# A second attention re-cast on the context's 64 columns: folded weights, raw contexts summed

## What is computed

```
x = x + tanh(g_xattn[0]) * attention0(layernorm(x), ctx)      # 16 heads, causal self part and cross part
x = x + tanh(g_ffn[0])   * moe_top2_capacity(layernorm(x))    # 8 experts, 320 slots each, F = 512
x = x + tanh(g_xattn[1]) * attention1(layernorm(x), ctx, ctx)
x = x + tanh(g_ffn[1])   * moe_dense(layernorm(x))            # 8 experts, all rows, F = 128

def attention1(query, key, value):          # one head of width 128, key and value are 64 wide
    q = query @ Wq + bq
    k = key @ Wk + bk
    v = value @ Wv + bv
    return softmax(q @ k.T, axis=-1) @ v
```

## Time and profile before

| | |
|---|---|
| time, median of 3 runs (lowest, highest) | 335.41 us (332.91 to 335.91) |
| the profiled execution: span from first to last instruction | 337.6 us |
| TensorE matmul busy in it | 312.9 us (93%) |
| TensorE weight load (overlaps) | 189.6 us (56%) |
| VectorE, ScalarE, GpSimd busy | 220.8, 194.1, 115.7 us |
| granted TensorE clock, mean | 0.995 |

### The profile page before, as it was taken

How to read it: one execution, slowest core, us unless ns; L and a number is a source line. 1 busy time by engine, 2 the same in 40 slices (tenths; PEclk the granted TensorE clock), 3 DMA queues, 4 the chain that set the end, 5 groups by cost and what they waited for, 6 DMA issues and landing times.

```text
span 337.6 us, 7474 instructions
## 1 busy us (share of the span) xinstructions
PE 312.9 (93%) x2891; PEld 189.6 (56%) x2891; DVE 220.8 (65%) x532; ACT 194.1 (57%) x410; POOL 115.7 (34%) x200
## 2 busy tenths in 40 slices
PE   8998969989999999899977999999996899999995
PEld 3545733334443434344666677777794357776665
DVE  4998798888989889676242052333321956779665
ACT  3468588978888889787266733323336265512221
POOL 6476732327334333231775003444442211110000
PEclk9999999999999999999997999999999999999999
DMA  7855995940437006240441580000002200000101
GB/s 174 199 110 160 175 213 132 209 90 10 153 110 209 5 5 188 70 124 2 109 157 35 133 212 10 21 18 19 22 12 70 71 0 2 1 2 0 31 3 31
DMA packets 35827, 27.83 MB, mean 82 GB/s; under 512 B 5627, under 2 KB 33070, under 8 KB 35792
## 3 DMA queue, kind: packets, MB, share of 16 engines
q1 hardware_dynamic: 33965, 25.04, 29.7%
q0 software_dynamic: 1280, 1.88, 1.7%
q10 hardware_dynamic: 547, 0.44, 0.5%
HBM read 11.89 MB, written 5.26 MB: 51 GB/s over the span
## 4 chain that ended last, share of the span: by engine, by line
PE 73%; ACT 7%; DVE 6%; issue 5%; POOL 5%; DMA 2%; SPq 0%; DVEq 0%; POOLq 0%; ACTq 0%
PE psum L1682 11%; PE psum L1876 11%; PE psum L1957 8%; PE psum L1624 5%; PE psum L1648 5%; PE psum L1945 4%; PE psum L1864 4%; ACT qk_r L948 3%; PE psum L1814 2%; POOL rows_in L797 2%; PE psum L1651 2%; PE psum L2060 2%; PE psum L2052 1%; PE psum L1575 1%; PE psum L1869 1%
## 5 line engine op out<-in xcount | busy, mean ns | idle before, releaser
L1213 DVE TENSOR_REDUCE nmax<-psum 128x2 f32<-128x1024 f32 (+2 forms) x88 | 102.0, 1216 | 11.6 <-PE psum L1624 10.3
L948 ACT ACTIVATE parts<-psum 128x512 f32<-128x512 f32 (+1 forms) x88 | 45.2, 566 | 8.6 <-PE psum L1648 7.7
L1876 PE MATMUL psum<-p_more,kcat 128*128 128x320 f32 (+2 forms) x160 | 40.2, 396 | 0.9 <-DVE p_more L1346 0.7
L819 POOL DMA_INDIRECT rows_back<-qcat,back_at x24 | 22.9, 952 | 50.3 <-ACT qcat L981 43.1
L1876 PEld LDWEIGHTS psum<-p_more,kcat 128*128 128x128 f32 x160 | 26.1, 190 | 9.1 <-issue 0.9
L1350 DVE TENSOR_TENSOR qcat<-psum,qk_r 128x320 f32<-128x320 f32 (+2 forms) x40 | 16.6, 422 | 22.1 <-ACT qk_r L989 13.5
L989 ACT ACTIVATE qk_r<-psum 128x320 f32<-128x320 f32 (+2 forms) x40 | 15.2, 384 | 24.5 <-PE psum L1876 21.5
L1682 PE MATMUL psum<-parts,v_aug 128*18 128x256 f32 (+1 forms) x352 | 28.5, 369 | 0.0
L1957 PE MATMUL psum<-h_t,kcat 128*128 128x512 f32 x60 | 28.1, 594 | 0.0
L1682 PE MATMUL psum<-qk_r,v_aug 128*18 128x256 f32 (+1 forms) x160 | 27.4, 373 | 0.0
L1648 PE MATMUL psum<-qcat,kcat 64*128 64x256 bf16 x256 | 24.7, 271 | 1.9 <-ACT p_more L948 0.8
(11 more groups left out here) (249 smaller groups left out, 630.4 us busy)
## 6 DMA issues: line engine op xcount, KB each, us to landing
kcat<-parts SPq DMA_DIRECT2D x18, 192.0 KB, 3.8
qcat<-parts SPq DMA_DIRECT2D x21, 128.0 KB, 3.6
kcat<-ones_b SPq DMA_DIRECT2D x8, 192.0 KB, 4.6
kcat<-in_L_ffn_wi_gate_dram SPq DMA_DIRECT2D x6, 256.0 KB, 4.5
kcat<-in_L_ffn_wi_up_dram SPq DMA_DIRECT2D x6, 256.0 KB, 4.8
kcat<-in_L_ffn_wo_dram SPq DMA_DIRECT2D x6, 256.0 KB, 5.0
parts<-in_L_ffn_w_dram SPq DMA_DIRECT2D x3, 512.0 KB, 5.6
rows_in<-zeros SPq DMA_DIRECT2D x1, 1290.0 KB, 5.7
```

The lines of the kernel that those rows point to most:

```text
L819: pool.indirect_dma_start(out=rows_back[:, :], out_offset=bass.IndirectOffsetOnAxis(ap=back_at[0:m, e, t:t + 1], axis=0), in_=eo[0:m, e % ...
L948: act.activation(p_slots[u % NPT][:, 0:w], s2_bank(s2_place[u])[:, 0:w], ACT.Exp, scale=SCALE).then_inc(p_in, 1)
L1213: dve.tensor_reduce(dst[:, :, n * g:n * (g + 1)], src.rearrange("p (r q k) -> p r q k", r=PAR, q=n), AX.X, ALU.max, negate=True).then_inc( ...
L1876: ins = pe.matmul(gate_up_bank(i, m)[:, 0:end - first], w_t[e][:, m, f * P:(f + 1) * P], xs_t[:, e % 2, first:end], start=True, stop=True)
```

## The change

Scores are q k.T = (h Wq + bq)(ctx Wk + bk).T. The change folds Wq Wk.T into one matrix of 128 x 64 (`mk`) with bq Wk.T as a bias column, so that a "query" has 64 numbers and is matched with the raw context; what is left of a query's score, the same for all its keys, is the offset h (Wq bk) + bq bk, which is computed for every tile (`off`, one column) and only rounds the subtracted maximum (`s1_bias`). On the other side p @ (ctx Wv + bv) = (p @ ctx) Wv + bv: the raw context rows are summed and then multiplied by Wv.

- `context` with its 8 banks and copies goes, and so do k1_t and v1. `fold_weights1` comes: two transposes, 2 unread matmuls, four small matmuls, three ScalarE instructions; then 8 unread matmuls (`N_UNREAD_ROWS`).
- The two tiles of a batch lie on rows 0 to 63 and 64 to 127: queries of odd tiles go to output partitions 64 on; the turned context is copied to partitions 64 to 127 by a DMA; `scores1(b)` does both tiles, each on its row half, into banks 0, 1 or 4, 5. `sums1(b)`: 4 x 2 matmuls, context rows (128 x 64) as weights, a tile's sums on each column half, into bank 6. `values1(b)`: one matmul of 256 columns of both tiles by a block-diagonal Wv (`w1_v2`), into bank 7.
- Each of ScalarE's `take_queries` has a second instruction for the offsets; VectorE gets a small instruction behind each maximum, and a copy of the sums (`take_sums1`).
- The order is now by batches on TensorE, ScalarE and VectorE. GpSimd gets a memset of w1_v2 among its constants, a scale of bv, and x + bv over all rows (into x1_sb) between rstd(2) and rstd(3). SyncE loads bv and Wv twice in place of two loads, and issues two DMAs (context rows again, and the copy of c_t) behind the loads of the last layer's weights.

```diff
-w1_v = sb("w1_v", [DC + 1, D])
+w1_v2 = sb("w1_v2", [P, 2 * D])
+b1v = sb("b1v", [P, D])
...
-c_t = sb("c_t", [DC + 1, NC * P])
+c_t = sb("c_t", [P, NC * P])
...
-k1_t = q_place(AFTER_HH + 6 * D, NC * P)
...
-v1 = q_place(AFTER_HH + 6 * D + NC * P, NC * D).rearrange("p (t d) -> p t d", t=NC)
...
+TURN1_BANK, MK_BANK = 3, 4
+N_UNREAD_ROWS = 8
+N_IN_LATE = 11
...
+def s1_bank(t):
+    return bank(4 * (t // QT % 2) + t % QT)
...
-        for w, n in ((w1_k, "k"), (w1_v, "v")):
-            load(w[0:DC, :], a["L1_xattn_W" + n])
-            load(w[DC:DC + 1, :], a["L1_xattn_b" + n].unsqueeze(0))
+        load(w1_k[0:DC, :], a["L1_xattn_Wk"])
+        load(w1_k[DC:DC + 1, :], a["L1_xattn_bk"].unsqueeze(0))
+        load(b1v[:, :], a["L1_xattn_bv"].partition_broadcast(P))
+        sp.wait_ge(w1v_zero, 1)
+        for t in range(QT):
+            load(w1_v2[t * DC:(t + 1) * DC, t * D:(t + 1) * D], a["L1_xattn_Wv"])
...
+    sp.dma_start(ctx_rows, c_in).then_inc(ctx_again, 16)
+    sp.dma_start(c_t[DC:2 * DC, :], c_t[0:DC, :]).then_inc(ctx_again, 16)
...
+    pool.memset(w1_v2[:, :], 0.0).then_inc(w1v_zero, 1)
...
+        link(pool.tensor_scalar(b1v[:, :], b1v[:, :], tanh_g[:, 1:2], None, ALU.mult))
...
     rstd(2)
+    pool.tensor_tensor(x1_sb[:, :, :], x_sb[:, :, :], b1v[:, :].unsqueeze(1).to_broadcast([P, NT, D]),
+                       ALU.add).then_inc(xv_in, 1)
     rstd(3)
...
-    for j in range(2 * B):
-        act.wait_ge(kv1_full, j + 1)
-        src = bank(KV1_BANK[j])
-        if j < B:
-            act.activation(k1_t[:, j * BANK:(j + 1) * BANK], src, ACT.Copy).then_inc(kv1_act, 1)
-        else:
-            dst = v1[:, CT * (j - B):CT * (j - B + 1), :]
-            act.activation(dst, src.rearrange("p (t d) -> p t d", t=CT), ACT.Copy).then_inc(kv1_act, 1)
+    act.wait_ge(gw_in, 1)
+    act.activation(bq_wide, zeros[:, 0:D], ACT.Identity, bias=b1_col[:, :]).then_inc(bq_in, 1)
+    act.wait_ge(mk_full, 1)
+    act.activation(w1_turned, bank(TURN1_BANK)[:, 0:D + DC + 1], ACT.Copy).then_inc(mk_act, 1)
+    act.wait_ge(mk_full, 2)
+    act.activation(mk, bank(MK_BANK)[:, 0:MK_OFF + 1], ACT.Copy).then_inc(mk_act, 1)
...
     def take_queries(s):
         first, end = BACK[s]
+        n = (end - first) // QT
         act.wait_ge(q1_full, s + 1)
-        act.activation(q1_of(first, end), bank(Q1_BANK)[:, 0:(end - first) * P], ACT.Identity,
-                       bias=b1_col[:, :]).then_inc(q1_act, 1)
+        act.activation(q1_t[:, first // QT:end // QT, :], bank(Q1_BANK)[:, 0:n * P]
+                       .rearrange("p (b q) -> p b q", b=n), ACT.Identity,
+                       bias=mk[:, MK_BIAS:MK_BIAS + 1]).then_inc(q1_act, 1)
+        act.wait_ge(off1_full, s + 1)
+        act.activation(s1_off[:, first:end], bank(OFF1_BANK)[:, 0:end - first], ACT.Identity,
+                       bias=mk[:, MK_OFF:MK_OFF + 1]).then_inc(off1_in, 1)
     def exp1(t):
+        b = t // QT
         act.wait_ge(nm1_in, t + 1)
-        if t >= 2:
-            act.wait_ge(p1t_full, t - 1)
-        act.activation(p1[:, t % 2, :], bank(t % 2), ACT.Exp, bias=s1_nmax[:, t:t + 1],
+        if b >= 2:
+            act.wait_ge(p1t_full, t - 2 * QT + 1)
+        act.activation(p1[:, b % 2, t % QT, :], s1_bank(t), ACT.Exp, bias=s1_bias[:, t:t + 1],
                        accum_out=s1_sum[:, t:t + 1]).then_inc(p1_in, 1)
     def take_turned1(t):
+        b = t // QT
         act.wait_ge(p1t_full, t + 1)
-        if t >= 2:
-            act.wait_ge(o1_full, t - 1)
-        act.activation(p1_t[:, t % 2, :], bank(2 + t % 2), ACT.Copy).then_inc(p1t_in, 1)
+        if b >= 2:
+            act.wait_ge(u1_full, b - 1)
+        act.activation(p1_t[:, b % 2, t % QT, :], bank(2 + t % 2), ACT.Copy).then_inc(p1t_in, 1)
     for e in range(E):
         take_weights1(e)
     take_rows(0)
     take_queries(0)
     take_rows(1)
-    exp1(0)
     take_queries(1)
-    for t in range(NT):
-        if t + 1 < NT:
-            exp1(t + 1)
+    for t in range(QT):
+        exp1(t)
+    for t in range(QT):
         take_turned1(t)
-        if t == ROWS_AT:
-            take_rows(2)
-        if t == QUERIES_AT:
-            take_queries(2)
+    take_rows(2)
+    take_queries(2)
+    for b in range(1, B):
+        for t in range(QT * b, QT * b + QT):
+            exp1(t)
+        if b > 1:
+            for t in range(QT * b - QT, QT * b):
+                take_turned1(t)
+    for t in range(NT - QT, NT):
+        take_turned1(t)
     dense_experts()
...
     def max1(t):
         dve.wait_ge(sc1_full, t + 1)
-        dve.tensor_reduce(s1_nmax[:, t:t + 1], bank(t % 2), AX.X, ALU.max, negate=True).then_inc(nm1_in, 1)
+        link(dve.tensor_reduce(s1_nmax[:, t:t + 1], s1_bank(t), AX.X, ALU.max, negate=True))
+        if t in (0, BACK[1][0], BACK[2][0]):
+            dve.wait_ge(off1_in, [first for first, _ in BACK].index(t) + 1)
+        dve.scalar_tensor_tensor(out=s1_bias[:, t:t + 1], in0=s1_nmax[:, t:t + 1], scalar=s1_off[:, t:t + 1],
+                                 in1=s1_off[:, t:t + 1], op0=ALU.subtract, op1=ALU.add).then_inc(nm1_in, 1)
+    def maxima1(b):
...
+    def take_sums1(b):
+        dve.wait_ge(u1_full, b + 1)
+        dve.tensor_copy(u1_t[:, b % 2, :], bank(U1_BANK)[:, 0:P]).then_inc(u1_in, 1)
+    def add_values(b):
+        dve.wait_ge(o1_full, b + 1)
+        if b == 0:
+            dve.wait_ge(xv_in, 1)
+        for t in range(QT * b, QT * b + QT):
+            dve.scalar_tensor_tensor(out=x1_sb[:, t, :], in0=bank(O1_BANK)[:, t % QT * D:(t % QT + 1) * D],
+                                     scalar=s1_rec[:, t:t + 1], in1=x1_sb[:, t, :],
+                                     op0=ALU.mult, op1=ALU.add).then_inc(x3_in, 1)
+        for t in range(QT * b, QT * b + QT):
             row_statistics(t)
-    def reciprocal1(t):
-        dve.wait_ge(p1_in, t + 1)
-        link(dve.reciprocal(s1_rec[:, t:t + 1], s1_sum[:, t:t + 1]))
-        link(dve.tensor_tensor(s1_rec[:, t:t + 1], s1_rec[:, t:t + 1], tanh_g[:, 1:2], ALU.mult))
+    def reciprocal1(b):
+        tiles = slice(QT * b, QT * b + QT)
+        dve.wait_ge(p1_in, QT * b + QT)
+        link(dve.reciprocal(s1_rec[:, tiles], s1_sum[:, tiles]))
+        link(dve.tensor_scalar(s1_rec[:, tiles], s1_rec[:, tiles], tanh_g[:, 1:2], None, ALU.mult))
...
     add_back(2, 1)
-    max1(0)
     statistics(2, 2, x_sb)
-    for t in range(NT):
-        if t + 1 < NT:
-            max1(t + 1)
-        reciprocal1(t)
-        if t == 0:
-            normalise(2, 2, x_sb)
-        if t >= 1:
-            add_values(t - 1)
-        if t == NT - 2:
-            normalise(3, 0, x1_sb)
-    add_values(NT - 1)
+    maxima1(0)
+    normalise(2, 2, x_sb)
+    maxima1(1)
+    reciprocal1(0)
+    take_sums1(0)
+    maxima1(2)
+    reciprocal1(1)
+    add_values(0)
+    maxima1(3)
+    take_sums1(1)
+    reciprocal1(2)
+    add_values(1)
+    normalise(3, 0, x1_sb)
+    take_sums1(2)
+    reciprocal1(3)
+    add_values(2)
+    take_sums1(3)
+    add_values(3)
...
-                    if e == 0:
-                        pe.wait_ge(kv1_act, 2 * B - 2)
                     pe.wait_ge(xt_in, e + 1)
                 if i == 1:
                     pe.wait_ge(wt_in[0], 3 * E)
-                    pe.wait_ge(kv1_act, 2 * B)
+                    pe.wait_ge(mk_act, 2)
...
-    def context(j):
-        if j >= 4:
-            pe.wait_ge(kv1_act, j - 3)
-        elif KV1_BANK[j] in W_LAST:
-            pe.wait_ge(wt_in[0], W_LAST[KV1_BANK[j]] + 1)
-        dst = bank(KV1_BANK[j])
-        if j < B:
-            ins = pe.matmul(dst, w1_k[:, :], c_t[:, j * SC:(j + 1) * SC], start=True, stop=True)
-        else:
-            for c in range(CT):
-                tok = (CT * (j - B) + c) * P
-                ins = pe.matmul(dst[:, c * P:(c + 1) * P], c_t[:, tok:tok + P], w1_v[:, :],
-                                start=True, stop=True)
-        ins.then_inc(kv1_full, 1)
-    for j in range(2 * B):
-        context(j)
+    def unread(n):
+        for _ in range(n):
+            pe.matmul(bank(0), ones_b[:, 0:P], ones_b[:, 0:BANK], start=True, stop=True)
+    def fold_weights1():
+        dst = bank(TURN1_BANK)
+        pe.transpose(dst[:, 0:D], w1_q[:, :], ident[:, :])
+        pe.transpose(dst[:, D:D + DC + 1], w1_k[:, :], ident[0:DC + 1, 0:DC + 1]).then_inc(mk_full, 1)
+        unread(2)
+        pe.wait_ge(mk_act, 1)
+        pe.wait_ge(bq_in, 1)
+        pe.wait_ge(wt_in[0], W_LAST[MK_BANK] + 1)
+        wq, wk, dst = w1_turned[:, 0:D], w1_turned[:, D:D + DC + 1], bank(MK_BANK)
+        pe.matmul(dst[:, 0:DC + 1], wq, wk, start=True, stop=True)
+        for t in range(QT):
+            pe.matmul(dst[t * DC:(t + 1) * DC, MK_BIAS:MK_BIAS + 1], wk[:, 0:DC], b1_col[:, :], start=True, stop=True)
+        pe.matmul(dst[:, MK_OFF:MK_OFF + 1], bq_wide, wk[:, DC:DC + 1], start=True, stop=True).then_inc(mk_full, 1)
+    fold_weights1()
+    unread(N_UNREAD_ROWS)
...
     def turn_back(s):
         first, end = BACK[s]
         if s > 0:
```

(103 more changed lines are left out.)

51 lines of the change are left out of this document (29 added, 22 removed).

## The result

| | before | after |
|---|---|---|
| time, median of 5 runs (lowest to highest) | 333.36 us (332.88 to 335.91) | 342.76 us (340.37 to 343.54) |
| ratio after to before | | 1.0254, 95% interval 1.0205 to 1.0303 |
| span of a profiled execution, mean clock | 337.6 us, 0.995 | 338.6 us, 0.988 |

The account below looks back on a forecast made before the run. TensorE was taken as the bound in the context's stage and second attention. Terms +0.5 - 2.45 + 1.65 = -0.3 on the 337.6 us span gave 337.3, less 2.2 to the plain runs' median: 335.1 us, range 331.8 to 338.9.

Parts of the forecast that it names:

- Step 2, the fold's -2.45: Context's stage: with the fold replacing the context's matmuls, the first row transpose starts 2.45 us earlier.
- rival D: Context's stage: the fold doesn't move the experts, giving 337.55 us; chance 0.05.
- Step 4, GpSimd's x + bv: Second attention: the addition costs nothing, or at most 0.5 us if it slows VectorE's normalising beside it.
- Step 4, the order: Second attention: walking through the engines' new instruction orders puts the dense start 1.65 us later.
- both gaps: Second attention: TensorE idles 1.7 us before sums1(1) (first gap) and 1.9 us before values1(2) (second gap).
- Step 3: Second attention: TensorE's own work falls by 2.3 us net, with halves running beside each other.
- Rival B: Second attention, scores1 and sums1: float32 halves don't overlap, +7.6 in place of +1.65, 341.05 us; chance 0.1.
- half form: Second attention: only the row halves run one after another, +4.0 us in place of +1.65.
- Rival C: Second attention: the waits are hidden and TensorE's sum of -2.3 counts, giving 331.15 us; chance 0.12.
- Step 1: Constants at 21 us: GpSimd's memset of w1_v2 is on the path and adds 0.5 us.
- Rival A: Before the fold's matmuls and at second-attention gaps: TensorE's clock falls, 1.7 us each; 336.8 or 338.5 us; chance 0.25.
- the sign of being right: Dense start 1.3 us behind its old distance from the gather, some 26.1 us after the first turned rows, not 24.5.

Follow-up runs that it names:

- b_again: The kernel before, unchanged, run and profiled a second time: 334.73 us, ratio 1.000.
- b_ctx: The kernel before with most of the context's key and value matmuls left out, copies kept: 337.83 us, ratio 1.010.
- rows17: The kernel after with 17 unread matmuls in place of 8 ahead of the first row transpose: 342.10 us, ratio 1.0238.
- rows30: The kernel after with 30 unread matmuls in place of 8 ahead of the row transposes: 342.30 us.
- xv_late: The kernel after with GpSimd's x + bv held back behind the fourth maximum: 339.55 us, ratio 1.0125.
- order2: The kernel after with x + bv late, 17 unread matmuls ahead of the row transposes, new orders on TensorE, ScalarE and VectorE: 331.91 us, ratio 0.994.
- no_off: The kernel after without the rows' offsets, their matmuls, copies and bias instructions: 339.93 us, ratio 1.013.
- order1: The kernel after with x + bv held back and VectorE's order alone changed: 338.38 us, ratio 1.010.
- xv_gaps: The kernel after with x + bv late, 17 unread matmuls ahead of the row transposes, and unread matmuls in three second-attention gaps: 335.70 us, ratio 1.007.

## Why the prediction was wrong, and where it was right

The sum was -0.3 us and +9.4 was measured. Of the 9.7 us between them the clock is some 5.2, a term that the sum had at nothing, the fold 2.4, GpSimd's addition 1.9 and the order 0.3; the memset, 0.2 too high, goes the other way.

**Step 2, the fold's -2.45: wrong, and the step that took the forecast's only gain away.** "L646 is issued at 185.97 and lands in 2.0 to 2.3 us, by 188.3, so it is not what ends last": the landing time was right, the start of the context's matmuls was not, since the row read for it came from an execution in which TensorE was late. In b_again's timeline the fold's 4.55 us end at 186.1, 2.2 us ahead of the landing. Measured against the landing, the gain is 0 (b_again, b_ctx, rows17, rows30). That was rival D, put at 0.05. The rows that warned stood in the first group: 1.48 of 3.45 us busy and a clock of 0.50 just ahead of the stage, and a span above every timed run. They were used for the price of a fall only.

**Step 4, GpSimd's x + bv at "nothing, ... at most 0.5": 1.9 us.** The addition starts the moment rstd(2) ends, together with the second bias instruction; the prediction had it from 270.8 on its time axis, beside VectorE's normalising, and bounded the harm by a slower instruction. The moment was right to 0.1 us (5.6 us behind the first turned rows); that the second bias instruction falls on the same moment was overlooked. The addition does not slow such an instruction, it stops it until the addition is over, whatever the size of what is stopped: one of 128 x 1 (after) and those of 128 x 2 (xv_late, order2) ended with it, and four of 128 x 128 took 3.15 us for 1.11 (no_off). The Trainium skill states this (SBUF — State Buffer, Who interferes with whom): VectorE and GpSimd share a pair of ports under an exclusive lock for a whole instruction, and VectorE needs it for two inputs in SBUF, or for a mode of one-input operations that tensor_scalar can enter, while a reduction on this chip never does. Every row here agrees: 2.31 us for the two-input form, 2.35 for tensor_scalar, 0.68 for a maximum. That maximum reads PSUM, so it alone does not tell the form from the place; the reciprocal of order2, 0.17 us from SBUF, does. By that rule the price was, as an estimate, the addition's whole length less what VectorE had to wait for anyway, up to 2.3 us, and it could have been had ahead of the result.

**Step 4, the order, +1.65: right in place and mechanism, 0.3 low.** xv_late has 26.48 - 24.51 = 1.97 us, both gaps are where the walk put them, with their releasers, at 1.44 and 1.73 us for 1.7 and 1.9, and a third of 0.4 us before values1(3). order1 gave 1.75 of it back by moving take_sums1(0) and normalise(3, 0), and order2 3.8, some 0.4 of it perhaps by its missing unread matmuls.

**Step 3, TensorE's own sum, -2.3: right.** 21.13 us busy at full clock against 23.39, so -2.26, and it does not count, as the step said. The halves overlap: from its start to the next instruction a pair of scores takes 1.06 us (263.15 to 264.21 in after), and two pairs in a row 1.91 (269.44 to 271.35 in order2), so 0.85 for the pair by itself and 0.2 for entering and leaving, for the 0.86 and 0.2 taken. Rival B is out. (Its half form was also summed wrong: four pairs at 0.86 more on the path are 3.4, so 1.65 + 3.4 = 5.1 and not 4.0.) Rival C (TensorE's sum counts in this stage) was false for the written order and nearly true for another: 24.5 - 2.3 = 22.2 against 22.72 in order2. Its 331.15 us is not confirmed by that, since it holds the fold's -2.45 as well.

**Step 1, the memset, +0.5: too high.** It took 0.31 us, not 0.55, and GpSimd's subtraction starts at 21.56 where b_again has 21.22. What became of these 0.3 us further on, no run shows.

**Rival A, the clock, left out of the sum: right in mechanism and in one of its two places, too cheap and too rare.** Behind the second gap there was a fall. The idle time ahead of the fold's matmuls (1.14 us) brought none by itself: rows17 keeps it (1.15 us) and stays at full clock there; the fall at 187.30 stands behind the wait for the rows, which the prediction did not have. One fall costs 1.6 to 2.0 us for the 1.7 reckoned. But it was priced at one or two falls with a chance of 0.25. After had a clock of 0.988 or less in every run: the two steps that failed made two further waits of some 2 us each, one ahead of the experts and one in turn1(0). The eight unread matmuls "against" it did not reach to the landing; seventeen nearly did, and the fall there was gone (rows17). "The gaps of step 4 lie between full stretches" did not hold either: a fall stands at 286.29.

**Span and median.** A time is the span plus 1.8 us. From 337.6 the sum of -0.3 should have led to about 339 us, or a start should have been made from a usual execution, some 333. The range has a slip of its own: half way to C's 331.15 is 333.1, not 331.8. And the sign of being right gives the stage twice, as 1.3 us longer (against the dense start in the trace) and as 26.1 for 24.5 (against that of the walk); the second is the forecast's +1.65.

## What to carry to other kernels

Before a step is put "on the path" from a profile in which the engine came late to it, ask when the next thing it needs would be there without it; here a load set by another engine's queue landed only 0.3 us before the end of work that nothing seemed to hide, and cutting 3.8 us of that work made the kernel 1% slower. A GpSimd addition on SBUF cost VectorE up to its whole length where VectorE had an instruction with two SBUF inputs or a float32 tensor_scalar at that moment: cut it in pieces or tie its start to a moment when VectorE's next instruction matters to nobody. And when a change cuts an engine's work but leaves the instruction orders to chance, walk through the orders with measured durations: nearly the same work in another order made the stage 3.8 us shorter.

## What was not expected of the hardware

- An instruction of one column was held 2.1 us by another engine's addition, and the trace books it as 2.31 us of VectorE busy, not as idle time: a group of eight such instructions with a mean of 0.48 us hides one.
- Less work on the busiest engine, with no wait instruction added, cost 3.4 us (b_ctx): the wait for the landing was 3.09 us, and 10.24 us at 1.2 GHz went with it.
- The falls differ between executions of the same kernel: rows17 ran at clocks of 0.973 to 0.989 and xv_gaps, which fills the same gap and three more and moves one addition, at 0.989 to 1.000. What share each single wait has in this was not tried.
